# Unit 0's front rebuilt in two attention layers with group norm (one Trainium2 core)

## What is computed

```python
xn = group_norm(x, gamma, beta)
q, k, v = (conv1x1(xn, w, b).reshape(B, N, C) for w, b in ((wq, bq), (wk, bk), (wv, bv)))
attn = jax.nn.softmax(jnp.einsum('bnc,bmc->bnm', q, k) * scale, axis=-1)
out = jnp.einsum('bnm,bmc->bnc', attn, v).reshape(B, H, W, C)
return conv1x1(out, wp, bp) + x
```

## Time and profile before

| | us |
|---|---|
| median of three runs (lowest, highest) | 252.61 (252.58, 252.69) |
| profiled execution, its own time | 254.9 |
| its span, first to last instruction | 253.1 |
| TensorE busy in it | 247.7 |
| VectorE busy | 187.3 |
| ScalarE busy | 149.4 |
| GpSimd busy | 125.2 |

### The profile page before, as it was taken

The page is one execution under the profiler, slowest core; times in us unless marked ns, Lnnn a source line. Parts: engine busy times, 40 slices in busy tenths (PEclk is TensorE's granted clock), DMA queues, the critical chain, the costliest instruction groups (busy, mean ns, idle before and its releaser), DMA issues.

```text
span 253.1 us, 4585 instructions
## 1 busy us (share of the span) xinstructions
PE 247.7 (98%) x1570; PEld 225.3 (89%) x1570; DVE 187.3 (74%) x490; ACT 149.4 (59%) x291; POOL 125.2 (49%) x151
## 2 busy tenths in 40 slices
PE   8899999999999999999999999999999999999995
PEld 6698889889998899889998899889998899889995
DVE  0279899988995788677885898687875788448804
ACT  2466434499995407930998607940998609740930
POOL 3010260388488605911597925911697927800870
PEclk9999999999999999999999999999999999999999
DMA  6999000000025001320034001320010001100112
GB/s 187 329 181 212 9 0 3 0 1 3 0 84 83 4 0 44 83 42 3 22 84 65 0 0 44 84 42 3 28 57 3 0 0 44 41 0 3 43 41 85
DMA packets 34767, 12.37 MB, mean 49 GB/s; under 512 B 26284, under 2 KB 34488, under 8 KB 34744
## 3 DMA queue, kind: packets, MB, share of 16 engines
q1 hardware_dynamic: 34720, 12.07, 19.5%
q10 hardware_dynamic: 24, 0.01, 0.0%
HBM read 7.88 MB, written 4.19 MB: 48 GB/s over the span
## 4 chain that ended last, share of the span: by engine, by line
PE 89%; DVE 6%; DMA 2%; issue 1%; ACT 1%; SPq 0%; DVEq 0%
PE ring L1133 12%; PE ring L1135 12%; PE ring L1134 12%; PE ring L1108 10%; PE ring L1107 10%; PE ring L1109 10%; PE ring L1080 3%; PE ring L1082 3%; PE ring L1081 3%; PE ring L1093 3%; PE ring L1095 2%; PE ring L1094 2%; DMA xnat<-in_x 2%; PE ring L947 2%; DVE R L732 2%; DVE xraw L593 1%
## 5 line engine op out<-in xcount | busy, mean ns | idle before, releaser
L363 POOL TENSOR_TENSOR P_lo<-S,P_hi 128x512 fp32r<-128x512 f32 x64 | 81.9, 1304 | 52.0 <-ACT S L503 51.9
L1133 PE MATMUL ring<-V,P_hi 128*128 128x258 f32 x256 | 72.7, 284 | 0.0
L1135 PE MATMUL ring<-V,P_lo 128*128 128x258 f32 x256 | 72.4, 283 | 0.0
L1134 PE MATMUL ring<-V,P_hi 128*128 128x256 f32 x256 | 72.3, 282 | 0.0
L502 ACT ACTIVATE P_hi<-S 128x512 fp32r<-128x512 f32 x64 | 40.3, 630 | 29.8 <-DVE S L791 29.8
L495 ACT COPY S<-ring 128x512 f32<-128x512 f32 x64 | 36.6, 590 | 31.3 <-PE ring L1109 29.4
L1107 PE MATMUL ring<-t_hi,xn_lo 128*128 128x512 f32 x128 | 49.9, 390 | 0.0
L1108 PE MATMUL ring<-t_lo,xn_hi 128*128 128x512 f32 x128 | 49.8, 389 | 0.0
L1109 PE MATMUL ring<-t_hi,xn_hi 128*128 128x512 f32 x128 | 49.8, 389 | 0.0
L1133 PEld LDWEIGHTS ring<-V,P_hi 128*128 128x128 f32 x256 | 48.5, 189 | 0.4
L1134 PEld LDWEIGHTS ring<-V,P_hi 128*128 128x128 f32 x256 | 48.4, 189 | 0.4
(11 more groups left out here) (117 smaller groups left out, 360.7 us busy)
## 6 DMA issues: line engine op xcount, KB each, us to landing
xnat<-in_x SPq DMA_DIRECT2D x8, 256.0 KB, 4.6
between<-xnat SPq DMA_DIRECT2D x16, 128.0 KB, 1.8
out<-xnat SPq DMA_DIRECT2D x16, 128.0 KB, 1.7
moved<-in_x SPq DMA_DIRECT2D x8, 128.0 KB, 4.4
moved<-between SPq DMA_DIRECT2D x16, 64.0 KB, 2.3
moved<-between SPq DMA_DIRECT2D x32, 32.0 KB, 1.9
w_wq<-in_L_conv_wq SPq DMA_DIRECT2D x2, 256.0 KB, 4.7
w_wk<-in_L_conv_wk SPq DMA_DIRECT2D x2, 256.0 KB, 4.6
```

Of the source, the lines that this page charges most:

```text
L363: nc.gpsimd.tensor_tensor(P_lo[:, exp_of(c, kb), :], S[:, tile_of(c, kb), :], P_hi[:, exp_of(c, kb), :].bitcast(F32), ALU.subtract).then_i ...
L1133: nc.tensor.matmul(bank[:, 0:C + 2], P_hi[:, tile, mine], v[:, kb, 0:C + 2], start=(kb == 0), stop=False)
L1134: nc.tensor.matmul(bank[:, 0:C], P_hi[:, tile, mine], v[:, kb, C + 2:VX], start=False, stop=False)
L1135: last = nc.tensor.matmul(bank[:, 0:C + 2], P_lo[:, tile, mine], v[:, kb, 0:C + 2], start=False, stop=(kb == NB - 1))
```

## The change

In unit 0 the pieces of x go to three banks (ring[2], ring[3], ring[6], ring[2]); VectorE's statistics read the bank, and ScalarE's copy to xraw comes after them. group_deviation and affine_map are rewritten with fused instructions, for all units. ScalarE's xn_high computes gain * xraw + shift itself and rounds it; VectorE computes the same unrounded into four tiles of S (normalise_first), and xn_low takes the difference. The product bv wp, the bias of the output, goes from TensorE to GpSimd (weighted_rows: ten instructions, ending in a rounded row and its rest), and two fp32r matmuls with a matrix of ones add it over the partitions to all of them; bp comes in with the `wide` load, which has three rows for two. Wx_product(0) writes to X; the third transposed weight of layer 2 to ring[6]. Two dummy matmuls are added behind the transposes of wk, four between mean and variance. The order of the front's second part is new on TensorE, ScalarE and VectorE: all three weights of layer 2 are transposed before the first t_product, A_product(1) stands between the two halves of t_product and Wx_product(1) behind them. The first t_product of a half in unit 0 runs the four matmuls with xn_hi first and those with xn_lo last.

```diff
@@ -14,7 +14,7 @@
-WIDE = VECTORS[3:5]
+WIDE = VECTORS[3:6]
@@ -347,6 +347,22 @@
+            def weighted_rows(l):
+                r = l * NV + VECTORS.index("bv")
+                pool.wait_ge(ld_w[l, "wp"], 16)
+                for k in range(KC):
+                    nc.gpsimd.tensor_scalar(weighted[:, l, k, :], w_raw[l, "wp"][:, k, :], vec_cols[:, k, r:r + 1],
+                                            None, ALU.mult).then_inc(po_bv, 1)
+                pool.wait_ge(po_bv, 5 * l + 2)
+                nc.gpsimd.tensor_tensor(weighted[:, l, 0, :], weighted[:, l, 0, :], weighted[:, l, 1, :], ALU.add
+                                        ).then_inc(po_bv, 1)
+                pool.wait_ge(po_bv, 5 * l + 3)
+                nc.gpsimd.tensor_copy(weighted_hi[:, l, :], weighted[:, l, 0, :]).then_inc(po_bv, 1)
+                pool.wait_ge(po_bv, 5 * l + 4)
+                nc.gpsimd.tensor_tensor(weighted_lo[:, l, :], weighted[:, l, 0, :], weighted_hi[:, l, :].bitcast(F32),
+                                        ALU.subtract).then_inc(po_bv, 1)
@@ -393,6 +409,8 @@
             power(0)
+            weighted_rows(0)
+            weighted_rows(1)
@@ -415,13 +433,15 @@
         def _(act):
...
-            def raw_rows(r, bank):
-                act.wait_ge(pe_xT, r + 1)
-                nc.scalar.copy(xraw[:, :, 2 * r * P:2 * (r + 1) * P], bank[:, :].rearrange("p (k n) -> p k n", k=KC)
+            def raw_rows(r):
+                act.wait_ge(dv_bn, r + 1)
+                nc.scalar.copy(xraw[:, :, 2 * r * P:2 * (r + 1) * P], rows_bank(r)[:, :].rearrange("p (k n) -> p k n", k=KC)
...
             def weight_transposed(l, n):
-                bank, dst = ((ring[4], wqT[:, l]), (ring[5], wkT_bk[:, l, :, 0:C]), (X, wvT[:, l]))[n]
+                bank, dst = ((ring[4], wqT[:, l]), (ring[5], wkT_bk[:, l, :, 0:C]),
+                             (ring[RING - 1] if l else X, wvT[:, l]))[n]
@@ -447,37 +467,37 @@
             def xn_high(v, q):
...
+                cols = slice(h * BANK, (h + 1) * BANK)
...
-                if v:
...
+                    nc.scalar.copy(xn_hi[:, k, cols], xraw[:, k, cols]).then_inc(ac_xh, 1)
...
-                    act.wait_ge(dv_xn, q + 1)
-                cols = slice(h * BANK, (h + 1) * BANK)
-                nc.scalar.copy(xn_hi[:, k, cols], xraw[:, k, cols]).then_inc(ac_xh, 1)
+                    act.wait_ge(dv_stat, SHIFT)
+                    nc.scalar.activation(xn_hi[:, k, cols], xraw[:, k, cols], ACT.Identity, bias=shift[:, k:k + 1],
+                                         scale=gain[:, k:k + 1]).then_inc(ac_xh, 1)
...
-            for r in range(NR):
-                raw_rows(r, ring[2 + r % 2])
-                if r == 2:
-                    A_high(0, 0)
+            raw_rows(0)
+            A_high(0, 0)
+            for r in range(1, NR):
+                raw_rows(r)
...
-            weight_transposed(1, 0)
-            weight_transposed(1, 1)
-            Wx_high(0, 0)
-            Wx_high(0, 1)
-            weight_transposed(1, 2)
...
-                A_high(1, k)
+                Wx_high(0, k)
+            weight_transposed(1, 0)
+            weight_transposed(1, 1)
...
             def t_high(u, h, k):
...
+                if u == 0:
+                    act.wait_ge(dv_att, k + 1)
@@ -502,9 +522,13 @@
-            for h in range(HALVES):
-                for k in range(KC):
-                    t_high(0, h, k)
+            t_high(0, 0, 0)
+            t_high(0, 0, 1)
+            weight_transposed(1, 2)
+            for k in range(KC):
+                A_high(1, k)
+            for k in range(KC):
+                t_high(0, 1, k)
@@ -584,10 +609,13 @@
             def statistics_of(v, r):
...
-                    dve.wait_ge(ac_xT, r + 1)
+                    dve.wait_ge(pe_xT, r + 1)
+                    for k in range(KC):
+                        last = nc.vector.bn_stats(bn[:, k, r, :], rows_bank(r)[:, 2 * k * P:2 * (k + 1) * P])
+                    last.then_inc(dv_bn, 1)
+                    return
...
-                    if v > 1:
-                        wait_for_x_low(dve, v - 1, TQ)
+                    wait_for_x_low(dve, v - 1, TQ)
@@ -620,16 +648,13 @@
-            def bias_columns():
-                dve.wait_ge(pe_ob, LAYERS)
-                for l in range(LAYERS):
-                    nc.vector.tensor_tensor(bias_col[:, l, :], bias_bank(l), vec_cols[:, :, l * NV + VECTORS.index("bp")],
-                                            ALU.add).then_inc(dv_oc, 1)
             def output_biases():
...
-                nc.vector.tensor_copy(out_bias[:, :, :], ring[RING - 1][:, :].rearrange("p (l c) -> p l c", l=LAYERS)
-                                      ).then_inc(dv_ob, 1)
+                for l in range(LAYERS):
+                    dve.wait_ge(ld_wide[l], 16)
+                    last = nc.vector.tensor_tensor(out_bias[:, l, :], ring[RING - 1][:, l * C:(l + 1) * C],
+                                                   wide[:, l, WIDE.index("bp"), :], ALU.add)
+                last.then_inc(dv_ob, 1)
@@ -640,13 +665,14 @@
             def group_deviation(v):
...
-                nc.vector.tensor_copy(gmean[:], mean_bank(v))
...
+                nc.vector.tensor_scalar(less_mean[:], mean_bank(v), -1.0, None, ALU.mult)
...
-                nc.vector.tensor_tensor(dev2[:], dev[:], dev[:], ALU.mult).then_inc(dv_stat, 1)
-                dve.wait_ge(dv_stat, at + DEV2)
-                nc.vector.tensor_tensor(var_c[:], dev2[:], mv[:, :, 1], ALU.add).then_inc(dv_stat, 1)
+                for k in range(KC):
+                    last = nc.vector.scalar_tensor_tensor(var_c[:, k:k + 1], dev[:, k:k + 1], dev[:, k:k + 1],
+                                                          mv[:, k, 1:2], ALU.mult, ALU.add)
+                last.then_inc(dv_stat, 1)
@@ -657,33 +683,38 @@
-                nc.vector.tensor_tensor(r0sq[:], r0[:], r0[:], ALU.mult).then_inc(dv_stat, 1)
+                for k in range(KC):
+                    last = nc.vector.scalar_tensor_tensor(r0sq[:, k:k + 1], r0[:, k:k + 1], r0[:, k:k + 1],
+                                                          var_e[:, k:k + 1], ALU.mult, ALU.mult)
+                last.then_inc(dv_stat, 1)
+                nc.vector.tensor_tensor(r0_gamma[:], r0[:], gamma, ALU.mult)
...
-                nc.vector.scalar_tensor_tensor(r_err[:], r0sq[:], -0.5, var_e[:], ALU.mult, ALU.mult
-                                               ).then_inc(dv_stat, 1)
-                dve.wait_ge(dv_stat, at + RERR)
-                nc.vector.scalar_tensor_tensor(rstd[:], r_err[:], 1.5, r0[:], ALU.add, ALU.mult).then_inc(dv_stat, 1)
-                dve.wait_ge(dv_stat, at + RSTD)
-                nc.vector.tensor_tensor(gain[:], rstd[:], gamma, ALU.mult).then_inc(dv_stat, 1)
+                nc.vector.tensor_scalar(factor[:], r0sq[:], -0.5, 1.5, ALU.mult, ALU.add).then_inc(dv_stat, 1)
+                dve.wait_ge(dv_stat, at + FACTOR)
+                nc.vector.tensor_tensor(gain[:], factor[:], r0_gamma[:], ALU.mult).then_inc(dv_stat, 1)
...
-                nc.vector.tensor_tensor(gain_mean[:], gain[:], gmean[:], ALU.mult).then_inc(dv_stat, 1)
-                dve.wait_ge(dv_stat, at + GMUL)
-                nc.vector.tensor_tensor(shift[:], beta, gain_mean[:], ALU.subtract).then_inc(dv_stat, 1)
...
+                for k in range(KC):
+                    last = nc.vector.scalar_tensor_tensor(shift[:, k:k + 1], less_mean[:, k:k + 1], gain[:, k:k + 1],
+                                                          beta[:, k:k + 1], ALU.mult, ALU.add)
+                last.then_inc(dv_stat, 1)
+            def normalise_first(q):
+                h, k = divmod(q, KC)
+                dve.wait_ge(ac_xT, 2 * (h + 1))
+                dve.wait_ge(dv_stat, SHIFT)
+                nc.vector.tensor_scalar(S[:, q, :], xraw[:, k, h * BANK:(h + 1) * BANK], gain[:, k:k + 1],
+                                        shift[:, k:k + 1], ALU.mult, ALU.add).then_inc(dv_xn, 1)
             def xn_low(v, q):
...
+                if v == 0:
+                    dve.wait_ge(dv_xn, q + 1)
...
-                nc.vector.tensor_tensor(xn_lo[:, k, cols], xraw[:, k, cols], xn_hi[:, k, cols].bitcast(F32),
-                                        ALU.subtract).then_inc(dv_xl, 1)
+                normal = xraw[:, k, cols] if v else S[:, q, :]
+                nc.vector.tensor_tensor(xn_lo[:, k, cols], normal, xn_hi[:, k, cols].bitcast(F32), ALU.subtract
+                                        ).then_inc(dv_xl, 1)
@@ -696,17 +727,14 @@
             affine_map(0)
-            normalise(0, range(0, 2))
-            Wx_low(0, 0)
-            xn_low(0, 0)
-            xn_low(0, 1)
-            attention_vector(0, 0)
-            attention_vector(0, 1)
-            normalise(0, range(2, 4))
-            bias_columns()
-            Wx_low(0, 1)
-            xn_low(0, 2)
-            xn_low(0, 3)
+            for q in range(2):
+                normalise_first(q)
```

(87 more changed lines are left out.)

43 lines of the change are left out of this document (19 added, 24 removed).

## The result

The changed kernel took 254.46 us (median of 8 runs, 253.84 to 255.57) and the kernel before, beside it, 252.63 (8 runs, 252.13 to 253.65): a ratio of 1.0067, 95% interval 1.0045 to 1.0088. The change makes it slower, by 0.7% or 1.8 us. I had forecast 250.4 in a range of 249.8 to 252.9.

The account below looks back on a forecast made before the run. TensorE, busy 98% of the span, bounds the kernel. With the early clock, V' 13.1 plus a stretch of 12.9 starts the scores at 26.0, 2.2 us sooner, off the 252.61 median: 250.4 us, range 249.8 to 252.9.

Parts of the forecast that it names:

- early-clock: TensorE rises from 1.2 to 2.4 GHz before 7.4 us; scores start at 26.0, 2.2 us sooner: 250.4, chance 0.42.
- V': End of unit 0's variance product on TensorE, 15.75 us before; forecast 13.1 with the early clock, 14.6 with the late.
- the price of nothing for GpSimd's ten instructions: GpSimd's bias work, 7.0 us from V' + 1.1, wanted at V' + 12.5, counted as hidden if VectorE is undisturbed.
- The base of the comparison: Sums made in the profiled execution, span 253.1 and time 254.9; the span's difference taken off the median of 252.61.
- the late clock: TensorE's clock rising between 10.2 and 12.3 us, as in the given profile; scores at 27.5, time 251.8.
- the rest that followed is now filled: Two keep_running fill TensorE's 0.84 us wait for x, so unbroken work from 1.10 may raise the clock before 7.4 us.
- rival 1: The clock doesn't come sooner despite the filled wait: 251.8 us (251.4 to 252.3), chance 0.28.
- The rebuilt front: TensorE's work up to the scores with the clock as before: V' 14.6, scores at 27.5, 0.7 us sooner.
- Rival 3: GpSimd stops VectorE from the power to xn_lo of quarter 1, 3.0 us: 253.4 early clock, 254.8 late; chance 0.14.
- the rule that speaks against the change: VectorE and GpSimd share ports, first comer holds them; GpSimd's ten instructions, starting with the affine map, would stop VectorE.
- The price of the stretch is thus 12.9: TensorE from V' to the scores: list of 12.69 us plus a 0.2 hole before the first t_product's xn_lo pieces.
- Behind the scores' start: VectorE enters the scores with about 1 us more lead, closing at most TensorE's 0.08 us hole; no new hole.

Follow-up runs that it names:

- second look: The kernel before, unchanged, run again beside the second group of kernels to catch a trace with TensorE's early clock: 252.48 us, ratio 0.9999.
- the version that beats both: Changed kernel; bv wp products on ScalarE, GpSimd's other six behind xn_low, real transposes for four dummies, A_product(1) before first t_product, xn_low 2 and 3 before t_low: 251.35 us.
- one whose rest was filled: The kernel before with only two dummy products added behind the transposes of wk, in TensorE's 0.84 us wait for x: 252.61 us, ratio 1.0003.
- the unchanged kernel beside the first group: The kernel before, run once more unchanged beside the first follow-up kernels, against runs of the same program at 252.41: 253.42 us, ratio 1.0048.

## Why the prediction was wrong

The early-clock executions side by side, from their traces (V' is the start of Wx_product(0), the next instruction):

| | V' | first t_product | scores | span | median |
|---|---|---|---|---|---|
| before (unchanged, second look) | 13.23 | 18.79 | 25.80 | 250.7 | 252.48 |
| after | 12.59 | 16.54 | 27.75 | 252.4 | 254.46 |
| after without GpSimd's ten | 12.39 | 15.75 | 25.63 | 250.3 | 252.09 |
| the version that beats both | 12.96 | 16.75 | 25.17 | 249.8 | 251.35 |

Two steps failed: the base from which the gain was taken, and the price of nothing for GpSimd's ten instructions. The first made the forecast a gain, the second made the measured time a loss.

**The base of the comparison** ("the difference in the span is taken off the median") put the forecast 2.3 us too low. The profiled execution took 254.9, the median was 252.61 with 0.11 between its lowest and highest run, and I had myself written that only 1.8 us lie around the span. So the runs of the median had spans of about 250.8, and whatever made the profile 2.3 us longer wasn't in them: it was the late clock, 2.4 us from one execution of before to the other (28.19 less 25.80). The sign was on the page before I began. Taken from the profiled execution instead, my span of 250.9 (253.1 less 2.2) gives 252.7 us with the 1.8 around it: no change. The 1.75 that remain to the measured 254.46 are those by which the scores start at 27.75 and not at 26.0.

**The clock** ("the rest that followed is now filled", 0.42 for the forecast against 0.28 for rival 1). The early clock is there in after, at about 6 us, but it is there in before too, within the first A_product, in the execution of the second look, and it stays away until 10.7 in one whose rest was filled. What I gave 0.42 to isn't an effect of the change. Rival 1 books no clock and lands at 251.8, near the 252.09 without GpSimd's ten, but for a wrong reason: it has the clock late in after, where it was early.

**The rebuilt front, contention aside.** Of the 0.7 us that I gave it, 0.17 is there (25.80 against 25.63). V' came somewhat sooner than forecast: 13.1 with the early clock, measured 12.4 to 12.6 (12.5 to 12.7 as the chain counts); statistics from the bank took 2.08 for six, against 2.15 from SBUF, so I was right to add nothing. But before's V' was at 13.23 in that state, so the gain is 0.84 and not the 1.15 of the case with the late clock. The stretch behind V' was mis-sized: TensorE's list was to grow by 0.25 (12.44 to 12.69) with a hole of 0.2 on top; both read from the start of Wx_product(0), it grew by 0.67, from 12.57 to 13.24, without a hole. What it is longer by is 0.19 in the two bias matmuls (0.65 from 24.98 to 25.63, for 0.46), 0.18 in the first half of t_product (3.16 from 15.75 to 18.91, where before takes 2.98) and 0.17 in the three transposes ahead of it (1.55 for 1.38); the two products of layer 2 give 0.09 back. The rewritten affine map gained nothing: from r0sq to the normalising it takes 1.25 us without GpSimd, where before's takes 1.17 (14.47 to 15.64) and I had 0.95. And moving the transposes of wq and wk behind the variance is a bad exchange by itself: 0.94 of real work in the waiting time were replaced by 0.98 of dummies.

**GpSimd beside VectorE** is the step that turned the sign. In the sum the ten instructions cost nothing ("Below that they are hidden, if they don't disturb VectorE"); the runs show 1.9 us behind V' and 2.2 in the medians. Rival 3 had the mechanism and the place, at a weight of 0.14, which was the mistake. I had the row and the rule that speaks against the change, and I saw that the ten instructions start together with the affine map on a path without slack; the price of nothing stood on a condition that the profile didn't support. Its own price of 3.0 was 1.1 too high, and that its 254.8 is near the measured 254.46 is luck: that figure goes with the late clock, and with the early one, which was there, it had 253.4 on the base that was too low. As for how it costs, "lets one GpSimd instruction of 0.74 slip in", at each of four dependent steps, is not what happened: the small steps lost 0.6 us together, and the large ones 0.57 (normalising) and 0.51 (two xn_low). GpSimd was itself dearer than my 0.70: a tensor_scalar takes 0.93 (though a cast 0.40), and two of the former take 2.92 beside VectorE.

**The order inside the front** ("The price of the stretch is thus 12.9", "a hole of 0.2 remains"). I checked its covers with undisturbed durations, and undisturbed they hold: no hole at all without the ten. That was no cushion, since the same ten instructions cost 0.7 in the old front and 2.2 in the new one. The moved matmuls were cover, and I had them down only as moved.

**Behind the scores' start** the forecast holds: 16.80 of 16.80, the 0.08 closed (the sum takes 0.1 for it in the case with the late clock and leaves it out in the other).

**The 0.2%** that I took for the finest difference is too fine where a program has executions of two lengths: ten runs of the unchanged kernel, four of them with spans of 252.6 and more, read 0.5% slow against 26 others of the same program.

Left open: what makes the clock of one program rise at 7 us in one execution and past 10 in the next. No row ahead of the rise differs in a way that I could name. The first rows of x are transposed at 6.0 to 6.9 us in the executions with the early rise and at 6.5 to 7.4 in those with the late one; the two overlap.

## What to carry to other kernels

Before anything is summed, take the time around the span from the profiled execution's own time and hold the rest against the median; where they don't fit, the profile shows another kind of execution, and a gain read from it may be in the median already. Work given to an idle GpSimd isn't free: list the VectorE instructions that will run beside it and ask how much of TensorE's list stands between them and their reader, for the price hangs on both. A filler in a waiting time is best real work, and pushing an instruction chain later pushes everything that hangs on it, here the residuals, into someone else's narrow place.

## What the runs showed of the hardware

- VectorE instructions of one or two elements a partition are stretched beside 128x256 instructions of GpSimd: two of them from 0.35 to 1.33 us beside residuals, `gain` from 0.16 to 0.41 beside weighted_rows. `factor`, a tensor_scalar with one tensor input, went from 0.17 to 0.31, and two normalisings of the same kind from 1.00 to 1.57. The Trainium skill, "SBUF — State Buffer", section "SBUF: two separate sides", has the lock for VectorE operations with two SBUF inputs or in a two-port mode; the runs agree for the first and show the loss for tensor_scalar too, without showing in which mode it ran or that the lock is the cause.
- GpSimd undisturbed, held back behind xn_lo: tensor_scalar with a column as scalar 128x256 float32 0.93 us (1.85 for two), tensor_tensor 0.74, cast to fp32r 0.40. ScalarE does the product of the first in 0.47 (0.94 for two).
- The first fp32r matmul of 512 columns behind float32 ones of 256 columns takes 0.42 us to the next (24.98 to 25.40 without the ten), behind float32 transposes of 128 columns 0.31 (15.75 to 16.06 there), where 0.23 is usual.
- A granted clock of 0.95 stood from 12 us to the end in the profile of the unchanged kernel beside the first group, and its 224.9 us behind the scores' start (252.6 less 27.7) are those of the executions at 1.00: here that column told nothing of the time.
